# Cross-attention of a decoder block on one Trainium2 core: scores on row halves from steps between keys, and denominators inverted in a 100x16 layout

## What is computed

```python
# 16 heads; q is absorbed into the 64-wide key space per head, kv_c is ctx (L=1444, 64)
kv_r = _apply_rope(kv_c, sin_k, cos_k)            # keys and values alike, (B, 1444, 64)
scores = q_absorbed @ kv_r.T                      # (B, 16 heads x 100 rows, 1444)
probs  = softmax(scores)
ctx    = probs @ kv_r                             # (B, 1600, 64)
out    = x + (ctx per head) @ (w_kc_kv, Wo)       # (B, 100, 256)
```

## Time and profile before

| | us |
|---|---|
| median of 3 runs | 2,810.13 |
| the profiled execution | 2,809.89 |
| its span | 2,807.7 |
| PE busy (94% of the span) | 2,641.3 |
| DVE busy (68%) | 1,903.4 |
| POOL busy (59%) | 1,643.6 |
| ACT busy (41%) | 1,152.6 |

### The profile page before, as it was taken

One profiled execution on the slowest core, in us unless ns is written; L12 is line 12 of the kernel. 1 busy time (PEld: TensorE's weight loads), 2 busy tenths in 40 slices (PEclk: granted clock), 3 DMA queues, 4 the chain that ended last, 5 costly groups with the idle time before them and its releaser, 6 DMA issues. The chain is left out here.

```text
span 2807.7 us, 41100 instructions
## 1 busy us (share of the span) xinstructions
PE 2641.3 (94%) x13650; PEld 1637.2 (58%) x13650; DVE 1903.4 (68%) x3015; ACT 1152.6 (41%) x1793; POOL 1643.6 (59%) x566
## 2 busy tenths in 40 slices
PE   6999769999979999999999999999999999999598
PEld 4545467777635555555555555555555555555388
DVE  6888755545377776777677767776777777774575
ACT  3323235555424444444444444444444444444143
POOL 1544513434417776777677767776777677767321
PEclk9999879999969999999999999999999999999799
DMA  4000032121210011001100110001101110100011
GB/s 120 19 18 23 12 110 48 41 52 42 58 31 20 21 26 35 20 20 25 35 20 20 25 32 23 20 25 31 24 20 25 27 28 20 25 18 3 25 42 41
DMA packets 56341, 89.07 MB, mean 32 GB/s; under 512 B 7163, under 2 KB 47311, under 8 KB 56161
## 3 DMA queue, kind: packets, MB, share of 16 engines
q1 hardware_dynamic: 56288, 88.40, 12.5%
HBM read 65.24 MB, written 23.14 MB: 31 GB/s over the span
## 5 line engine op out<-in xcount | busy, mean ns | idle before, releaser
L1434 POOL TENSOR_TENSOR x_acc<-x_acc,x_prob 120x1600 f32<-120x1600 f32 (+1 forms) x320 | 1156.9, 3615 | 282.6 <-ACT x_prob L1450 278.8
L1543 DVE TENSOR_REDUCE x_mx<-x_ring 124x1 f32<-124x480 f32 (+3 forms) x1248 | 784.6, 658 | 425.1 <-PE x_ring L1653 424.5
L1450 ACT ACTIVATE x_prob<-x_scores 120x800 f32<-120x800 f32 (+1 forms) x768 | 633.8, 840 | 919.4 <-PE x_scores L1600 912.7
L1612 PE MATMUL x_context<-x_prob,x_kv 120*64 120x400 f32 (+1 forms) x3072 | 654.1, 519 | 0.0
L1597 PE MATMUL x_scores<-x_qa,x_ka 128*120 128x400 f32 (+1 forms) x1536 | 551.5, 359 | 0.0
L1600 PE MATMUL x_scores<-x_qb,x_kb 128*120 128x400 f32 (+1 forms) x1536 | 530.3, 345 | 0.0
L1653 PE MATMUL x_ring<-x_ka,x_qa 128*124 128x480 f32 (+3 forms) x1248 | 516.8, 437 | 3.1 <-DVE x_mx L1543 1.1
L1653 PEld LDWEIGHTS x_ring<-x_ka,x_qa 128*124 128x124 f32 (+1 forms) x1248 | 220.0, 186 | 321.9 <-issue 161.8
L1597 PEld LDWEIGHTS x_scores<-x_qa,x_ka 128*120 128x120 f32 (+1 forms) x1536 | 279.7, 182 | 107.3 <-issue 60.6
L1434 POOL TENSOR_TENSOR x_acc<-x_prob 121x1600 f32<-121x1600 f32 x32 | 155.3, 4853 | 248.8 <-ACT x_prob L1450 248.8
L1612 PEld LDWEIGHTS x_context<-x_prob,x_kv 120*64 120x64 f32 (+1 forms) x3072 | 167.0, 135 | 227.6 <-issue 162.9
(11 more groups left out here) (167 smaller groups left out, 2928.5 us busy)
## 6 DMA issues: line engine op xcount, KB each, us to landing
x_qraw<-scratch_qp SPq DMA_DIRECT2D x64, 400.0 KB, 5.1
scratch_qp<-q_qs SPq DMA_DIRECT2D x32, 400.0 KB, 3.7
x_raw<-in_ctx SPq DMA_DIRECT2D x32, 360.0 KB
a_x<-in_x SPq DMA_DIRECT2D x8, 400.0 KB
scratch_x<-a_x SPq DMA_DIRECT2D x8, 400.0 KB
q_x<-scratch_x SPq DMA_DIRECT2D x8, 400.0 KB
x_xr<-scratch_x SPq DMA_DIRECT2D x32, 100.0 KB
scratch_x<-x_x SPq DMA_DIRECT2D x32, 100.0 KB
```

The lines of the kernel that those rows point to most:

```text
L1434: pool.tensor_tensor(acc[0:rows, parity], first, prob[0:rows, c % PR], ALU.add).then_inc(acc_done.sem, 1)
L1450: act.activation(prob[0:rows, c % PR, u * HALF:(u + 1) * HALF].rearrange("p (j s) -> p j s", j=2), psc[0:rows, u, :, 0:BANK], ACT.Exp).the ...
L1543: dve.tensor_reduce(mx[0:block_rows(r), r, i:i + 1], ring[0:block_rows(r), bank, 0:b - a], AX.X, ALU.max).then_inc(rg.read[bank], 1)
L1612: mm = pe.matmul(pav[DC * s:DC * s + DC, j, 0:BANK], kv[0:rows, parity, c], prob[0:rows, c % PR, cols], start=c == 0, stop=c == LC - 1)
```

## The change

Queries (`phase_queries`): ACT's copy of the absorbed queries becomes a rounding copy of all 128 partitions (two heads at a time) and DVE takes the remainder, so that SP stores rounded queries and remainders (`qh`, `ql`), in four transfers for one. The keys' rotation moves here: per batch SP loads the context rows, POOL makes three products and a sum, DVE the difference between each chunk and the one before it (`kdiff`), and SP stores the rotated keys (`kr`) and the differences (`kd`).

Cross-attention: PSUM keeps the scores of a chunk, and the next chunk adds only (keys of c+1 − keys of c) times queries to them; the row of maxima is added once, in chunk 0. Every operand has 64 rows, and the two column blocks j of a half u stand on partitions 0 to 63 and 64 to 127 of the operands, so that their matmuls use two row halves of the array. Maxima are taken per side t from rounded keys and queries: 7 blocks of 115 queries x 3 spans x 2 sides = 42. Keys and steps come from memory twice, beside each other (`kr`, `kd`, pieces of 64 elements), and need six transposes. The order of the units is a new list. Reciprocals go over memory. The core of the diff:

```diff
 # phase_queries, pool
+            def rope_products(k, i):
+                pool.wait_ge(k_loaded[i % 2].sem, k_loaded[i % 2].at(k, 32 * (i // 2 + 1)))
+                wait(pool, k_rotated.sem, k_rotated.at(k, i))
+                half = DC // 2
+                pool.tensor_tensor(kt1[:], kraw[:, i % 2], cosk[:], ALU.mult).then_inc(k_terms.sem, 1)
+                for to, frm in ((slice(0, half), slice(half, DC)), (slice(half, DC), slice(0, half))):
+                    pool.tensor_tensor(kt2[:, :, to], kraw[:, i % 2, :, frm], sink[:, :, to],
+                                       ALU.mult).then_inc(k_terms.sem, 1)
...
                 for p in range(HP):
                     rotate_middle(k, p)
                     if p == 1 and more:
                         rows_rstd(k + 1)
+                    if p % 2 == 0:
+                        rope_products(k, p // 2)
+                    else:
+                        rope_sum(k, p // 2)
 # phase_queries, vector
+            def key_steps(k, i):
+                dve.wait_ge(k_rotated.sem, k_rotated.at(k, i + 1))
+                wait(dve, k_stored[(i + 1) % 2].sem, k_stored[(i + 1) % 2].at(k, 32 * ((i + 1) // 2)))
+                dve.tensor_tensor(kdiff[:], krot[:, i % 2, 1:LC], krot[:, i % 2, 0:LC - 1],
+                                  ALU.subtract).then_inc(k_diffed.sem, 1)
...
 # phase_cross_attention, the order
+        pairs = iter([[("max", t, r, i) for t in range(2)] for r in range(MB) for i in range(3)])
+        for c in range(LC):
+            if c == 0:
+                order.append([("kT", 2), ("out",), ("context",), ("scores", 0), ("scores", 1), ("dT", 0), ("dT", 1)])
+                continue
+            count = 0 if c == LC - 1 else 3 if c == 1 else 2
+            own = [("scores", 0)]
+            own += next(pairs) if count > 0 else []
+            own += [("scores", 1)]
+            own += [u for _ in range(count - 1) for u in next(pairs)]
+            own += [("dT", 2)] if c == 1 else [("mT",), ("kT", 0), ("kT", 1)] if c == LC - 1 else []
+            own += [("context",)]
+            own += [("den", c - 4)] if c in (4, 5) else []
+            order.append(own)
...
 # sync
+            def invert(n):
+                bank, value = rg.place(n, ("den", 1))
+                sp.wait_ge(rg.read[bank], value)
+                sp.dma_start(d["den"].rearrange("(s n) -> s n", s=2), dens[0:DC + 1:DC].rearrange("s j n -> s (j n)")
+                             ).then_inc(den_stored.sem, 16)
+                sp.wait_ge(den_stored.sem, den_stored.at(n, 16))
+                sp.dma_start(few[:], d["den"].rearrange("(a b) -> a b", b=H)).then_inc(den_loaded.sem, 16)
+                sp.wait_ge(den_inverted.sem, den_inverted.at(n, 1))
+                sp.dma_start(d["rden"].rearrange("(a b) -> a b", b=H), few[:]).then_inc(rden_stored.sem, 16)
+                sp.wait_ge(rden_stored.sem, rden_stored.at(n, 16))
+                for s in range(2):
+                    sp.dma_start(rden[DC * s:DC * s + DC].rearrange("e j n -> e (j n)"),
+                                 d["rden"][s * HALF:(s + 1) * HALF].unsqueeze(0).broadcast_to([DC, HALF])
+                                 ).then_inc(rden_loaded.sem, 16)
+            def slot(n, parity):
...
+                    load_kv(n + 1, 1 - parity)
+                    load_q(n + 1, 1 - parity)
+                    if not is_at(n, B - 2):
+                        load_kr(n + 2)
...
+                    load_xr(n, parity)
...
                     store_x2(n - 2, parity)
+                    load_kd(n + 2)
+                invert(n)
+                if not last and not is_at(n, B - 2):
+                    load_qm(n + 2)
+                if not last:
+                    load_m(n + 1, 1 - parity)
 # vector
+            def invert(n):
+                dve.wait_ge(den_loaded.sem, den_loaded.at(n, 16))
+                dve.reciprocal(few[:], few[:]).then_inc(den_inverted.sem, 1)
...
+                    if c == 7:
+                        invert(n)
+                    if c >= LC - 2:
+                        normalise(n, c - (LC - 2))
 # tensor
-                pe.matmul(out, ka[:, parity, a:a + rows], qa[:, parity, cols], start=True, stop=False)
...
-                mm = pe.matmul(out, kb[:, parity, a:a + rows], qb[:, parity, cols], start=False, stop=True)
...
+                for k, q in ((dh, qh), (dl, qh), (dh, ql)):
+                    last = c > 0 and q is ql
+                    for j, part in enumerate(halves):
+                        mm = pe.matmul(psc[0:rows, u, j, 0:BANK], k[part, parity, a:a + rows], q[part, parity, cols],
+                                       start=c == 0 and k is dh and q is qh, stop=last,
+                                       skip_group_check=c > 0)
+                if c == 0:
...
+                    for j, part in enumerate(halves):
+                        mm = pe.matmul(psc[0:rows, u, j, 0:BANK], onerow[part, 0:rows], mq[part, parity, cols],
+                                       start=False, stop=True)
...
+                    mm = pe.matmul(ring[0:block_rows(r), bank, 0:b - a], qm[part, r * MR:r * MR + block_rows(r)],
+                                   kh[part, a:b], start=True, stop=True)
```

More of the change, by code:

```diff
@@ new lines, in phase_cross_attention, with made, made_at @@
+        assert next(pairs, None) is None
+        is_unit = lambda u: u[0] not in ("scores", "context")
+        beside = [[u for u in own if is_unit(u)] for own in order]
+        units = [u for own in beside for u in own]
+        def made(n, u):
+            if u[0] == "kT":
+                return n + (2 if u[1] < 2 else 1) <= B - 1
+            return n <= B - 2 or u[0] in ("out", "den")
+        def made_at(n, u):
+            return made(n, u) if isinstance(n, int) else True
+        ends = [(n,) + u for n in (B - 2, B - 1) for u in units if made(n, u)]
@@ L1441, in _ @@
             act.sem_inc(exp_done.sem, exp_done.credit)
+            for bank in range(2):
+                act.sem_inc(rg.read[bank], rg.credit)
             def exponentials(n, c, u):
@@ L1562, in slot @@
-                    if c == C_M - 1 and more:
-                        for i in (1, 2):
-                            bank, value = rg.place(n, ("max", MB - 1, i))
+                        elif u[0] == "dT":
+                            low_steps(n, 1 - parity, u[1])
+                        elif u[0] == "max":
+                            maximum(n, u[1], u[2], u[3])
+                        elif u[0] == "mT":
+                            turn_maxima(n)
+                    if c == LC - 2 and not is_at(n, B - 1):
+                        for t in range(2):
+                            bank, value = rg.place(n, ("max", t, MB - 1, 2))
@@ L1573, in _ @@
             output(B, 0)
+            invert(B)
             for j in range(2):
@@ L1604, in context @@
-            def context(n, parity, c, j):
+                cols = slice(u * BANK, (u + 1) * BANK)
+                halves = [slice(DC * j, DC * j + DC) for j in range(2)]
+                pe.wait_ge(exp_done.sem, exp_done.at(n, 2 * c + u - 1))
+                if c == 0 and u == 0:
+                    pe.wait_ge(q_loaded.sems[parity], q_loaded.done(n, parity))
+                    bank, value = rg.place(n - 1, ("dT", 2))
+                    pe.wait_ge(rg.read[bank], value)
+                for k, q in ((dh, qh), (dl, qh), (dh, ql)):
[4 more added lines that the diff above has]
+                                       skip_group_check=c > 0)
@@ new lines, in context, with turn @@
+                for j in range(2):
+                    for s in range(2):
+                        cols = slice(s * HALF + j * BANK, s * HALF + (j + 1) * BANK)
+                        mm = pe.matmul(pav[DC * s:DC * s + DC, j, 0:BANK], kv[0:rows, parity, c],
+                                       prob[0:rows, c % PR, cols], start=c == 0, stop=c == LC - 1)
+                mm.then_inc(av_done.sem, 1)
+            def turn(bank, i, chunk):
+                a = span[i][0]
+                for c in range(4 * i, 4 * i + 4):
+                    rows, b = rows_of(c), start_of(c) - a
+                    mm = pe.transpose(ring[:, bank, b:b + rows],
+                                      chunk(rows, c), ident[0:rows, 0:rows])
+                return mm
@@ L1648, in make @@
                 elif u[0] == "max":
-                    if u[1] == 0 and u[2] == 0:
-                        pe.wait_ge(q_low.sem, q_low.at(n, 1))
-                    a, b = span[u[2]]
-                    r = u[1]
-                    mm = pe.matmul(ring[0:block_rows(r), bank, 0:b - a],
-                                   qa[:, 1 - parity, r * MR:r * MR + block_rows(r)], ka[:, 1 - parity, a:b],
-                                   start=True, stop=True)
+                    t, r, i = u[1:]
+                    if r == 0 and i == 0 and t == 0:
+                        pe.wait_ge(qm_loaded.sem, qm_loaded.at(n + 1, 32))
+                        for k in range(3):
```

(9 more changed lines are left out.)

511 lines of the change are left out of this document (286 added, 225 removed).

## The result

| | before | after |
|---|---|---|
| median, us | 2,810.07 (4 runs, 2,808.9 to 2,810.5) | 2,967.81 (4 runs, 2,965.5 to 2,968.6) |
| ratio to before, 95% interval | | 1.0561 (1.0542 to 1.0579) |
| span of the profiled execution | 2,807.7 | 2,966.1 |
| mean granted clock | 0.971 | 0.954 |
| DMA engines' busy share over the span | 12.5% | 29.4% |

The account below looks back on a forecast made before the run. PE's work was taken as the bound, the ring close behind. To 2,810 us, slots add 127, query stage 4, stage start 2, tail 5: 2,948 us; own range 2,890 to 3,040, 8 in 10 from 2,810 to 3,190.

Parts of the forecast that it names:

- The chunk: Chunks 2 to 10 of a slot: 4.26 us each, the second pair of maxima waiting for the two-bank ring.
- the saved work reaches the end: Faster rival: second pair of maxima does not wait, slot 47 to 49 us, kernel 2,573, halfway 2,700; chance 0.18.
- break-even: For the faster rival: a chunk of 3.85 us, a ring wait of 0.6.
- Row halves: Scores matmuls in pairs on two row halves run beside each other, 0.18 us a pair; scores −4.0 us a slot.
- The rival in which they run one after another: Scores pairs on row halves cost 0.37 us, not 0.18: 235 us more, 3,180; chance 0.14, half-overlap included.
- The prediction's estimate from that page's figure for a load: Scores: 0.1 us a load of 120 columns, 0.2 a pair, making the slot about 0.3 us longer.
- The slot: One batch of cross-attention: 60.2 us against 56.1, +4.1, in slots 0 to 30: +127 us.
- the clock falls: Rival: granted clock falls to 0.50, 1.2 GHz, as where PE waits most; beyond 3,500 us; chance 0.02.
- chunks 11 to 1: In a slot: chunks 11 and 0 take 12.4 us, chunk 1 with three pairs of maxima 7.3.
- Denominators: 2.1 us a slot; their way over memory covered in the slot, +5 in the tail.
- Query stage: POOL and DVE gain work but stay below PE's 44 us a group; +4 us, bounds −2 and +40.
- Stage start: Start of cross-attention: three more maxima, rotation gone, larger first loads: +2 us.

Follow-up runs that it names:

- experiment 1: Kernel after with each chunk's context matmuls cut into two column halves and a pair of maxima between them: 2,808.2 us, ratio 0.9994 to before.
- experiment 2: Kernel after with the 42 maxima of a slot reading only 8 columns of each filled bank: 2,599.8 us, ratio 0.9261 to before.
- experiment 3: Kernel after with six score matmuls issued as three of one row half, then three of the other: 2,973.2 us, ratio 1.0581 to before.
- experiment 9: Kernel after with reciprocals of 128x400 taken straight from the ring, without the way through memory: 3,166.1 us, ratio 1.1280 to before.
- experiment 4: Kernel after with VectorE taking the key steps one head pair later in the query stage: 3,018.7 us, ratio 1.0750 to before.
- Experiment 6: Kernel after with GpSimd's key rotation cut from 768 numbers a row to 64: 2,944.1 us, ratio 1.0484 to before.
- experiment 11: Experiments 10's version with half of the middle rotations moved to VectorE, taking two of ScalarE's four copies a head pair away: 2,708.7 us, ratio 0.9644 to before.
- experiment 7: Kernel after with the key steps taken by GpSimd behind its sum instead of VectorE: 2,966.1 us, ratio 1.0557 to before.
- Experiment 8: Kernel after with steps on GpSimd, context split around the pairs and a new unit order, step transposes spread over chunks 0 to 2: 2,808.9 us, ratio 0.9999 to before.
- experiments 10: Experiment 8 with each pair's maxima set apart around six score matmuls and denominators in the middle of chunks 3 and 4: 2,732.3 us, ratio 0.9724 to before.

## Why the prediction was right, step by step

*The chunk.* Right in size (4.26 forecast, 4.24 measured) and in reason: the second pair waits for the ring, with the context behind it. Experiments 1 and 2 took the wait away by order and by shorter reads, and the chunk fell to 3.55 and 3.28. The rival "the saved work reaches the end" was right on what is saved and wrong on whether it arrives; its break-even, a chunk of 3.85, did not hold: experiment 1 has a chunk of 3.55 and takes as long as the kernel before (2,808.2 us), because the query stage (+26), a dearer chunk 11 (11.4 against 10.2 us) and the clock (10.2) take the rest.

*Row halves.* Forecast 0.18 a pair, and 0.18 it is. The rival in which they run one after another is out, even where they are issued so (experiment 3). The Trainium skill ("TensorE: Matmul & The Clock Gate", What overlaps and what doesn't), which the prediction names, has loads beside running matmuls only where the row group differs. The trace has more: each half starts a matmul every 0.18 us and its loads last 0.18 us each, so a load lies beside a matmul of its own half too. The prediction's estimate from that page's figure for a load, 0.1 us each and 0.2 a pair, is not what the starts show, and its 0.3 us a slot does not follow from 0.02 a pair, which over 74 pairs would be 1.5.

*The slot.* 60.2 forecast, 60.46 measured, and that they agree so closely is partly luck: without a fall of the clock a slot takes 59.4, and the falls add 1.1 on average. In the slot of 59.36, chunks 11 to 1 took 19.9 us (forecast 12.4 + 7.3), chunks 2 to 10 with the denominators 39.5 (38.4 + 2.1), of which the denominators 1.3. The rival "the clock falls" had 0.02 and a price for a slot at 1.2 GHz throughout; what came was a fall of 3.4 us in three slots of four, which it did not name. The granted clock in the rows before was 1.00 throughout the slots and 0.50 where PE waited most, and that was read as all or nothing.

*Denominators.* Forecast to be covered in the slot and +5 in the tail. In the slot DVE never waits for them, and the tail grew by 3.2. What the forecast did not price is the other side: in this order of the ring, reciprocals of 128x400 would have cost 198 us (experiment 9).

*Query stage.* This is the step that failed: +26 against +4. It gave GpSimd 39 us a group and DVE 31 to 37, and concluded that both stay under PE's 43.9 (a window; by PE's starts a group took 44.4). Measured, a group lasts 47.5 us in the mean, with GpSimd 42 (295 / 335 × 47.5) and DVE 35: each alone still under PE's. But DVE's subtraction, with two SBUF operands, and GpSimd's instructions did not go on beside each other: with GpSimd 88% busy, the 0.9 us subtraction took 2.5 us in the mean (32 of them 80.8 us), and GpSimd's next instruction often 0.67 more. Behind six of them, of 6.35 us each, PE waited for DVE's rotations, 15 us in all. In experiment 4 such a step took up to 13.3. The price per operation that the forecast took, 1.0 to 2.6 us, was right in the mean; that it is a wait that stops everything behind it on DVE was missed. Experiment 6 gave back 23.7 us by easing GpSimd alone, experiment 11 gave 23.6 by easing GpSimd and ScalarE. The Trainium skill ("SBUF — State Buffer", Who interferes with whom) has the rule that was needed: a VectorE instruction with two SBUF inputs contends with a GpSimd one that reads SBUF, and the loser blocks; the traces agree, with either engine as the loser, and add that VectorE can stay blocked over ten further GpSimd operations in a row.

*Stage start.* +8.2 against +2. PE waited 3.0 us for the first doubled load of keys, and the maxima of the first batch come in pairs every 1.50 us as at the half clock before, three more of them, with the first denominators among them. With reads of 8 columns (experiment 2) the same stretch took 50.8 us in place of 61.1, so the reads of the maxima hold it too; how the 8 us divide was not tried.

## What to carry to other kernels

Work saved on an engine that shares a two-bank ring with its reader reaches the end only if the order leaves the reader's time between two fills; here the same work in another order was worth 160 us. Before work is moved to GpSimd or VectorE, count not only each one's busy time but the VectorE operations that have all their operands in SBUF: beside unbroken GpSimd work each can be held for one of GpSimd's instructions or for ten, and everything behind it waits with it. Waits of one or two us that return in every round can cost more than their own length: 113.7 us of them came with 198 in experiment 9, and with 70 falls of the granted clock.

## What was not expected of the hardware

- A VectorE subtraction of 121x704 with both operands in SBUF: 0.89 us alone, 12.61 us while GpSimd ran without a gap; cut to 64 columns its longest was still 5.7. In after, 24 of 32 got in behind one GpSimd instruction (1.4 to 1.7 us) and six behind five (6.35). Beside GpSimd's long sums (3.6 us each) a multiply got in at the end of a sum (2.76 and 3.74 us, experiment 1). A normalisation of 100x256 within SBUF went from 0.40 to 1.10 us in the same way (experiment 7).
- The granted clock fell to 1.2 GHz for 3.4 us at a time, 23 times in after behind the waits of chunk 1. It fell 70 times in experiment 9, with waits of 1.8 to 1.9 us more in each of chunks 5 and 6, 6 times in experiment 1, in chunk 11 behind the wait of 1.8 us there, and never in the slots of experiments 2, 8, 10 and 11. Experiment 8 kept the full clock with its waits of 0.6 and 0.8 us, and experiments 10 and 11 did with one of 1.5 us in each slot, in chunk 0. So the falls come and go with where the waits stand, and not with their length alone; what it takes was not tried, and 8 of the 31 slots of after kept the full clock with the same waits.
- Matmuls on the upper row half start before earlier-issued ones on the lower half (experiment 3).
